# Loading the second attention's slot 1 a stage earlier, and the FFN's transposes between the output products

## The reference, cut to what matters

```python
x = x + attn_a(layernorm(x), Wq, Wc, Wk, Wv, Wo)        # 32 heads of 16, low-rank k and v, rotary, no mask
x = x + ffn(layernorm(x), lora_A, lora_B, W, bias, lw)  # one linear map with a LoRA term
x = x + attn_b(layernorm(x), w_attn, b_attn, w_proj, b_proj)  # causal, alibi, 32 heads of 16
x = x + ffn(layernorm(x), lora_A, lora_B, W, bias, lw)
# attn_b, per batch:
q, k, v = split(x @ w_attn + b_attn)
scores = q k^T / 16 + slope_h * (pos_k - pos_q), -inf above the diagonal
out = (softmax(scores) @ v) @ w_proj + b_proj
```

## Time and profile before

| what | value |
|---|---|
| three runs, median | 1810.11 us (1803.03 to 1814.71) |
| profiled execution | 1811.41 us |
| its span | 1809.6 us |
| mean granted TensorE clock | 0.955 |
| first attention | about 184 to 883 us of the span |
| "mid" | 886 to 1176 us |
| second attention | 1179 to 1680 us |
| "fin" | 1683 to 1804 us |

### The profile page before, as it was taken

The page is one execution under the profiler, slowest core; times in us unless marked ns, Lnnn a source line. Parts: engine busy times, 40 slices in busy tenths (PEclk is TensorE's granted clock), DMA queues, the critical chain, the costliest instruction groups (busy, mean ns, idle before and its releaser), DMA issues. The chain is left out here.

```text
span 1809.6 us, 32945 instructions
## 1 busy us (share of the span) xinstructions
PE 1662.6 (92%) x13040; PEld 857.5 (47%) x13040; DVE 1390.8 (77%) x3007; ACT 973.4 (54%) x1103; POOL 142.8 (8%) x224
## 2 busy tenths in 40 slices
PE   6898999999999999999889998959999999999697
PEld 4554333333333333333246677624545454554486
DVE  3776799999999999999176444727898989885585
ACT  3432377777777777777421111124666666667210
POOL 3332200000000000000000000030000000003000
PEclk9999699999999999999989999957999999999799
DMA  6776334333333333330532246463464554542221
GB/s 215 222 176 198 65 65 89 62 60 65 55 55 55 55 58 54 55 54 11 167 109 71 69 140 189 128 113 56 89 100 74 92 83 82 89 76 68 98 75 70
DMA packets 116857, 167.58 MB, mean 93 GB/s; under 512 B 20828, under 2 KB 58092, under 8 KB 116588
## 3 DMA queue, kind: packets, MB, share of 16 engines
q1 hardware_dynamic: 114880, 160.17, 39.0%
q0 software_dynamic: 1824, 5.31, 1.4%
HBM read 100.41 MB, written 64.50 MB: 91 GB/s over the span
## 5 line engine op out<-in xcount | busy, mean ns | idle before, releaser
L354 DVE TENSOR_REDUCE mxp<-ps_m 128x1 f32<-128x512 f32 x1280 | 799.5, 686 | 70.6 <-PE ps_m L320 64.9
L671 ACT ACTIVATE a_p<-a_ps_s 128x1024 f32<-128x1024 f32 x512 | 522.9, 1026 | 148.8 <-PE a_ps_s L591 136.6
L671 ACT ACTIVATE b_p<-b_ps_s 128x1024 f32<-128x1024 f32 (+1 forms) x320 | 295.0, 939 | 188.2 <-PE b_ps_s L591 184.8
L351 DVE CUSTOM_DVE_ANT_0 ps_m<-ps_m,b_masks 128x128 f32<-128x128 f32 (+3 forms) x512 | 240.3, 518 | 77.1 <-PE ps_m L320 74.4
L320 PE MATMUL ps_m<-slot_qk 62*128 62x512 f32 (+3 forms) x624 | 239.2, 468 | 28.6 <-DMA slot_qk<-alibi_rows 17.0
L320 PE MATMUL ps_m<-a_slot_qk 62*128 62x512 f32 x640 | 238.2, 450 | 0.8
L591 PE MATMUL a_ps_s<-a_slot_qk 64*128 64x512 f32 x640 | 232.3, 443 | 1.2
L615 PE MATMUL a_ps_o<-a_p,a_slot_v 128*32 128x256 f32 x2560 | 205.6, 390 | 9.9 <-ACT a_p L671 5.4
L591 PEld LDWEIGHTS a_ps_s<-a_slot_qk 64*128 64x128 f32 x640 | 96.2, 185 | 128.9 <-issue 123.1
L591 PE MATMUL a_ps_s<-slot_qk 64*128 64x512 f32 x384 | 136.2, 454 | 0.6
L320 PEld LDWEIGHTS ps_m<-slot_qk 62*128 62x128 f32 x624 | 106.2, 200 | 59.3 <-DVE mxp L354 27.0
(11 more groups left out here) (209 smaller groups left out, 2294.5 us busy)
## 6 DMA issues: line engine op xcount, KB each, us to landing
va_groups<-w_o SPq DMA_DIRECT2D x16, 512.0 KB, 3.7
ka_parts<-pa_parts SPq DMA_DIRECT2D x16, 512.0 KB, 3.9
qa_parts<-pa_parts SPq DMA_DIRECT2D x32, 256.0 KB, 3.7
kb_parts<-slot_memory SPq DMA_DIRECT2D x16, 512.0 KB, 3.5
qb_parts<-slot_memory SPq DMA_DIRECT2D x32, 256.0 KB, 3.9
vb_groups<-w_proj SPq DMA_DIRECT2D x16, 512.0 KB, 3.2
a_slot_qk<-qa_parts SPq DMA_DIRECT2D x60, 128.0 KB, 4.2
a_slot_qk<-ka_parts SPq DMA_DIRECT2D x48, 128.0 KB, 6.9
```

The lines of the kernel that those rows point to most:

```text
L351: dve.tensor_tensor_reduce(from_, from_, mask_of_query[:, CHUNK - keys:], 1.0, LOWEST, ALU.add, ALU.max, accum_out=to).then_inc(piece_take ...
L354: dve.tensor_reduce(to, from_, AX.X, ALU.max).then_inc(piece_taken, 1)
L671: act.activation(p_sb[:, (2 * u + pair) % NP, :, off:CHUNK], ps_s[:, 2 * pair:2 * pair + 2, off:CHUNK], ACT.Exp, scale=scale).then_inc(exp ...
```

## The change

1. **Slot 1 of the second attention is loaded in "mid".** It gets memory of its own, shared with buffers that are free by then (`second_qk` beside the first FFN's normed and turned tokens, `second_v`). POOL clears it when the last FFN product is complete, and SyncE loads group 1 into it by shares in the last chunk, after each share's stores. In the attention only slot 2 is cleared and loaded at the start, and the 48 pieces of step 0 lie in all ten units, as in the other steps; TensorE waits for slot 1 by `wait_loaded` before the first.
2. **The order of the FFN stages.** In step k: two of the four o tiles, the f transposes, the other two o tiles. With it the list `order` changes, and so the bank of each task. The wait for the o operand stands ahead of the transposes.
3. **Finer waits.** The first product on turned tokens waits, piece by piece, for each of its four turned pieces, where before it waited for all four: the latent product of the first projection, f, and the first qk product.

```diff
-    SKIP = 3 if AT_ONCE else 0
-    before_unit_of_first = [0] * SKIP + [2 * round(NPC * sum(columns[SKIP:u]) / sum(columns[SKIP:]) / 2)
-                                         for u in range(SKIP, NU + 1)]
-    crow, rows = first.crow, first.rows
+    READY = len(ready)
+    crow, rows = ready[0].crow, ready[0].rows
...
             if i == 0:
-                if j:
-                    pe.wait_ge(rows_set[j - 1], SETS)
-                    pe.wait_ge(first_loaded[j - 1], K_LOAD)
-                wait_past(pe, qk_loaded[j], loads(g) * LOAD - (K_LOAD if j else 0))
+                if j >= READY:
+                    pe.wait_ge(rows_set[j], SETS)
+                    pe.wait_ge(first_loaded[j], K_LOAD)
+                elif g:
+                    slots[j].wait_loaded(pe)
+                wait_past(pe, qk_loaded[j], loads(g) * LOAD - (K_LOAD if j >= READY else 0))
...
                 early.stores.wait(pool, B)
-                for g in range(1, SLOTS):
-                    slots[g].clear(pool, cleared)
-                pool.wait_ge(cleared, 1)
-                slots[1].load_k(pool, k_d, 1, alibi_d, first_loaded[0])
+                for g in range(READY, SLOTS):
+                    slots[g].clear(pool, cleared[g])
+                pool.wait_ge(cleared[READY], 1)
+                slots[READY].load_k(pool, k_d, READY, alibi_d, first_loaded[READY])
...
-                begin(1)
+                begin(READY)
...
                     for u in range(NU):
-                        before = before_unit if s else before_unit_of_first
-                        lo, hi = AHEAD + before[u], AHEAD + before[u + 1]
+                        lo, hi = AHEAD + before_unit[u], AHEAD + before_unit[u + 1]
...
-def split_products(pe, out, lhs, rhs, pieces, between=None):
+def split_products(pe, out, lhs, rhs, pieces, between=None, before_piece=None):
...
+        if before_piece and (a, b) == (0, 0):
+            before_piece(kc)
         mm = pe.matmul(out, lhs[a](kc), rhs[b](kc), start=(n == 0), stop=(n == len(steps) - 1))
...
-                for task in turn_tasks[c]:
-                    banks.wait_drained(pe, task)
                 task = ("latent", c)
...
     for k in range(STEPS):
+        if k < NC:
+            order += [("o", k, t) for t in range(TPC // 2)]
         if 0 <= k - 1 < NC:
             order += f_turns[k - 1]
         if k < NC:
-            order += [("o", k, t) for t in range(TPC)]
+            order += [("o", k, t) for t in range(TPC // 2, TPC)]
...
+                        if c == NC - 1:
+                            if i == 0:
+                                sp.wait_ge(second.cleared, 1)
+                            second.load_share(sp, i, 1, env["qb_d"], env["kb_d"], env["vb_d"],
+                                              env["alibi"], env["ones"])
...
             for k in range(STEPS):
+                def products(tiles):
+                    natural("o", k, o_parts if fast else [output.o_sb[:, k % 2]], w_out, tiles=tiles)
+
+                if k < NC:
+
+                    pe.wait_ge(o_split if fast else output.o_scaled, KC * (k + 1))
+                    products(range(TPC // 2))
                 if 0 <= k - 1 < NC:
                     f_norm.transposes(pe, banks, k - 1, f_turns[k - 1], ident)
                 if k < NC:
-
-                    pe.wait_ge(o_split if fast else output.o_scaled, KC * (k + 1))
-                    natural("o", k, o_parts if fast else [output.o_sb[:, k % 2]], w_out)
+                    products(range(TPC // 2, TPC))
...
                 if 0 <= c < NC:
-                    for task in f_turns[c]:
-                        banks.wait_drained(pe, task)
-                    natural("f", c, f_xnt, w_eff)
+                    natural("f", c, f_xnt, w_eff, turns=f_turns[c])
                 c = k - 2
                 if nxt and 0 <= c < NC:
                     if c == 0:
                         pe.wait_ge(w_split, KC)
-                    for task in q_turns[c]:
-                        banks.wait_drained(pe, task)
...
+                if nxt and k == NC + 1:
+                    banks.wait_full(pool, ("f", NC - 1, TPC - 1))
+                    second.clear(pool, second.cleared)
...
+        ffn_at = at_here()
+        ffn_memory = sb("ffn_memory", [P, Slot.QK_WORDS])
+        second_qk = also("second_qk", ffn_at, Slot.QK_WORDS)
...
+        second_b = Slot(second_qk, second_v[:, :], True)
```

More of the change, by code:

```diff
@@ L149, with __init__, attention_plan @@
 class Early:
-    def __init__(self, nc, ctx, tag, causal, consts, first, ps_m, rows, stores, pieces_early):
+    def __init__(self, nc, ctx, tag, causal, consts, ready, ps_m, rows, stores, pieces_early):
         self.pieces, self.stores = pieces_early, stores
-        attention_plan(self, nc, ctx, tag, causal, consts, first, ps_m, rows)
-def attention_plan(early, nc, ctx, tag, causal, consts, first, ps_m, rows_of_maxima):
+        attention_plan(self, nc, ctx, tag, causal, consts, ready, ps_m, rows)
+def attention_plan(early, nc, ctx, tag, causal, consts, ready, ps_m, rows_of_maxima):
     def block(qh, kt):
@@ L408, in pieces_from @@
             if lo == 0:
-                first.wait_loaded(pe)
+                slots[0].wait_loaded(pe)
                 if causal:
@@ L452, in run @@
             slots.extend(more)
-            for n in range(SLOTS - 1 - len(more)):
+            for n in range(SLOTS - READY - len(more)):
                 slots.append(Slot(sb(f"slot_qk{n}", [P, Slot.QK_WORDS], F32R),
@@ L466, in run @@
             v_loaded = [sem(f"v_loaded{j}") for j in range(SLOTS)]
-            cleared = sem("cleared")
+            cleared = {g: sem(f"cleared{g}") for g in range(READY, SLOTS)}
             score_ready = sem("score_ready")
@@ L996, in _ @@
                             if share < PT:
-                                first.load_share(sp, share, env["qa_d"], env["ka_d"], env["va_d"], None, env["ones"])
+                                first.load_share(sp, share, 0, env["qa_d"], env["ka_d"], env["va_d"], None, env["ones"])
                     if c == 0 and i == 0:
@@ L1051, in _ @@
                 split_products(pe, banks.out(task)[0:LATENT, :], [lambda kc: wc_high[:, kc, :], lambda kc: wc_low[:, kc, :]],
-                               x_parts, KC).then_inc(banks.fill(task), 1)
+                               x_parts, KC, None, lambda kc: banks.wait_drained(pe, turn_tasks[c][kc])
+                               ).then_inc(banks.fill(task), 1)
                 query(0)
@@ L1322, in scale, with output_and_ffn @@
                               ALU.mult).then_inc(self.o_scaled, 1)
-def output_and_ffn(nc, env, tag, output, w_out, out_bias, nxt, w_eff, early, first=None):
+def output_and_ffn(nc, env, tag, output, w_out, out_bias, nxt, w_eff, early, first=None, second=None):
     x_sb, w, consts = env["x_sb"], env["w"], env["consts"]
@@ L1472, in between, with natural @@
                 return maxima if c == NC - 1 else None
-            def natural(kind, c, lhs, weights, cols=slice(0, D)):
-                for t in range(TPC):
+            def natural(kind, c, lhs, weights, cols=slice(0, D), tiles=range(TPC), turns=None):
+                for t in tiles:
                     task = (kind, c, t)
@@ L1479, in natural, with turned @@
                     tokens = slice(t * P, (t + 1) * P)
+                    def turned(kc):
+                        if turns and t == tiles[0]:
+                            banks.wait_drained(pe, turns[kc])
                     if len(weights) > 1:
@@ L1514, in _, with turned @@
                         banks.wait_empty(pe, task)
+                        def turned(kc):
+                            if m == 0:
+                                banks.wait_drained(pe, q_turns[c][kc])
                         at = (m + KC) % PT * P
@@ L1518, in _ @@
                                        [lambda kc, x=x: x[:, kc, :] for x in q_xnt], KC,
-                                       between(c, m)).then_inc(banks.fill(task), 1)
+                                       between(c, m), turned).then_inc(banks.fill(task), 1)
                     natural("v", c, q_xnt, w_qkv, slice(2 * D, 3 * D))
```

83 lines of the change are left out of this document (47 added, 36 removed).

## The result

| | before | changed |
|---|---|---|
| median | 1811.12 us (1803.03 to 1814.71, 4 runs) | 1784.12 us (1779.97 to 1787.05, 4 runs) |
| profiled execution | 1811.41 us | 1787.05 us |
| its span | 1809.6 us | 1785.2 us |
| mean granted clock | 0.955 | 0.967 |

The ratio of the times is 0.9855, with a 95% interval from 0.9816 to 0.9895: the changed kernel is 1.5% faster. The forecast was 1790, with a range from 1773 to 1806. All medians and ratios in this document are of fast runs; the one slow run, `skip3`'s of 1863.79 us, is left out.

The account below looks back on a forecast made before the run. TensorE, busy 1662.6 of 1809.6 us, was taken as the bound. Terms -18.8 + 0.3 + 1.5 - 3 - 1.5 + 1.0 = -20.5 against 1811.4 gave 1790.9, set to 1790 for the runs' median; range 1773 to 1806.

Parts of the forecast that it names:

- Step 1: Second attention's first step: no wait for slot 1, half clock throughout, 67.5 us becoming 48.7, so -18.8; slot 2's loads hidden.
- Rival B: Second attention's first step: clock returns midway, since the start is denser; 7.5 to 11.5 us more gained; chance 0.22.
- Step 2: Middle stage's last chunk: slot 1's loads raise DMA share to about 0.7 and delay stores; 0 to +2, taken +0.3 us.
- Step 3: Middle stage's new order: 9.4 us gained are lost before f, whose bank frees late; half clock there costs +1.5 us.
- Step 4: Finer waits: -3 us in the middle stage's last chunk, -1.5 us in the first projection.
- Step 5: Last stage's new order: transposes +1.8, new waits +2.6, end wait -1.9, half clock spared -1.5; +1.0 us in all.

Follow-up runs that it names:

- skip3: The changed kernel with the old spread of the second attention's first-step pieces, none in units 0 to 2; 1798.40 us, ratio 0.9906.
- front7: The changed kernel with the second attention's first-step pieces in units 0 to 6, none in the last three; 1795.71 us, ratio 0.9922.
- adds_first_mid: The changed kernel, but in the second step of "mid" DVE adds the o products to x before scaling the next chunk; 1775.49 us, ratio 0.9799.
- clear_early: The changed kernel with POOL's clearing of slot 1 ahead of the last norm's power of -1/2 instead of behind it; 1778.61 us, ratio 0.9806.
- before_again: The kernel before, unchanged, profiled once more; one execution, 1802.53 us.
- late_slot1: The kernel before with the new order and finer waits, slot 1 still cleared and loaded in the attention; 1808.59 us, ratio 0.9979.

## Why the prediction was right, and where it wasn't

**The total** lay 6 us from the forecast and within its range, but partly by luck: the second attention was forecast 13.3 us too long, and the rest 9.5 us too short.

**Step 1, slot 1 loaded early: the wait, right; the clock, wrong.** The stall of 17 us went, and slot 2's loads were hidden, as forecast. "I therefore take half clock through the step" failed: it lasted 16 us of 34.6, in place of 48.7. Rival B named this outcome and priced it at 7.5 to 11.5 more; it was 14.1 (48.7 - 34.6). The step's error was to read one execution as the rule. The row with TensorE busy for 40.44 of 40.51 us at 0.50 belongs to one execution of a program that in another was back at full clock 9.7 us behind the stall, and to a spread of the pieces that the change itself removed. Had the spread stayed, 48.7 would have been close in two of three executions (48.0 and 40.6 in those of `skip3`, 46.7 in `front7`). I priced the removed stall and counted the spread as mere filling of gaps (-0.3), while it was worth about 10 us. That this is the clock is shown; why the clock returns earlier with the even spread is not. The Trainium skill ("TensorE: Matmul & The Clock Gate", What's actually happening) has it that sustained activity lifts the throttle. The traces agree in part: with the even spread the clock was back 12 to 17 us after the start in seven executions, but in `front7` TensorE was busy for 40.30 of 40.50 us and the clock was not back until their end.

**Step 2, the loads in the last chunk: right in that they hide, but its clearing was not priced.** The DMA share rose to 0.67 over 42 us, as forecast, and from the first pieces to the attention TensorE took 52.9 us, with 52.6 and 53.2 in the kernel before. The clearing was given no price. It costs DVE 3.2 us (1.92 to 5.08) and TensorE 0.7 to 1.6 in the two pairs of runs above. Two rows in the timeline of the kernel before could have told, POOL's clearing of slot 0 behind the norm one chunk earlier, and DVE's scaling beside it:

```profile
1043.91 3.52 POOL L114 MEMSET o_qk<- 128x4096 f32 x1
1044.00 5.08 DVE L846 TENSOR_SCALAR mid_q_xn<-x_sb,mid_q_mv,mid_q_rstd 128x512 f32<-128x512 f32 x4 [1.12 <-POOL mid_q_rstd L851]
```

Whoever adds a second such clearing can read its price off the first. The Trainium skill ("SBUF — State Buffer", Who interferes with whom) has the rule: GpSimd and VectorE share a pair of ports, a VectorE instruction such as tensor_scalar in a two-port mode and a GpSimd one exclude each other, and the second blocks until the first is done; a tensor_tensor with both inputs in SBUF contends only with a GpSimd instruction that reads there. By that rule the clearing would cost up to its own length in front of the scaling and nothing beside the additions, and both traces agree (+3.2 us of 3.52, and 2.49 unchanged).

**Step 3, the order in "mid": right.** f started 42.1 us after the stage's first product, 41.9 before; the bank was the cause, as `adds_first_mid` showed. The half clock cost 1.9 us, forecast +1.5: from the first f product to the next step's first product TensorE took 15.6 us instead of 13.7.

**Step 4, the finer waits: the mechanism right, the size off, and in the last chunk hidden by something else.** The forecast there was a wait of about 3 us; it was 6.24. What the finer wait itself is worth can be read from DVE's addition behind the store of v to TensorE's first piece: 4.89 to 4.91 us in the three traces with the coarse wait, 3.12 to 3.16 in the ten with the finer one. That is 1.75 us, where the term was 3. The sum had compared TensorE's start behind four subtractions (1126.13) with the end of one (1124.0), and left out the 0.4 us from that end to TensorE's start. And the half clock behind the wait, for which 0.9 of the 3 stood, was not spared: the clock was 0.50 in the first 2 us of the pieces in all ten. What outweighed the 1.75 us is the store of v: DVE waits 2.9 us longer for it, by the clearing and by what stays open above. In the first projection the term was -1.5: the wait of 2.14 became 1.81, released by POOL's split of a weight, which was ready right behind the old releaser. It was 1.60 in `front7` and 0.59 to 1.01 in eight other executions, so the profiled one was the unluckiest.

**Step 5, "fin": the mechanism right, some sizes off.** The term +1.8 for the transposes came as 1.9, the new waits of 1.1 and 1.5 us as 1.04 and 1.10, and the wait at the end fell by 1.9, as forecast. The stretch behind that wait became 1.0 us shorter, where 1.5 stood for the half clock (12.8 us in the changed kernel, 13.75 before; 11.25 in seven other traces with the finer wait, where all of it was spared). What had no term: the second step's o products start 0.6 us later after the stage's first, and about 0.9 us more goes between them and the last wait, about half of it as more half clock in the 10 us behind the long wait. Net +2.6 against +1.0, within its ends; the other traces with this order give -0.1 to +3.2 against the same 117.8, so the +2.6 is one draw.

## What to carry to other kernels

A reordering that fills a wait gains nothing while the resource that the next product needs, here a PSUM bank, is freed behind the same slow event; list for each moved product the bank, who drains it, and what that engine does first. A one-off operation on an idle engine isn't free: look which instruction of another engine it lies beside. And one profile gives one draw of the clock: before a term is built on a stretch at half clock, ask what else the change does to the mix of work in it, and look at the spread of the runs (1803.03 to 1814.71 us in four runs of the kernel before, 1801.01 to 1820.37 in 19 others, 1779.97 to 1787.05 in four of the changed one).

## What the runs showed of the hardware

- A MEMSET of 128x4096 on GpSimd (3.52 us) stretched four TENSOR_SCALAR of 128x512 on VectorE from 1.92 to 5.08 us wherever they began together (seven profiles for slot 1's clearing, the kernel before for slot 0's). Four TENSOR_TENSOR of 128x512 beside it, in `clear_early`, kept their 2.49 us.
- Behind the same stall at the same instructions, the clock returned after 9.7 and 10.5 us in two executions (`before_again`, `late_slot1`) and after 40 us in a third (the kernel before). Without a stall it returned 12 to 17 us after the attention's start with the pieces spread evenly, and 20.5 to 43.5 us after it with the pieces in seven units. TensorE was busy for 0.97 or more of each of these stretches at half clock, and for 0.99 or more in two of some 10 us (`before_again`, `late_slot1`) as in two of some 40 (the kernel before, `front7`). What tells them apart is open.
